# Attention and expert kernel: one burst of value products per batch, with scores and the projection issued ahead of it

## The chip, the cores and the metric

The kernel runs on one core of a Trainium2 chip. The metric is the device time in microseconds (us) of one execution. Three executions of the kernel before gave 748.78, 749.50 and 751.17 us, median 749.5. The profile is of another execution, which took 750.0 us; the span from its first to its last instruction is 748.1 us.

## What is computed

The input is x (64 batches, 64 channels, 256 positions) and a context of the same shape. First cross attention over channels is added to x, then a mixture of experts:

```
q = rotary(Wq @ layernorm(x) + bq);  k = rotary(Wk @ ctx + bk);  v = Wv @ ctx + bv
scores = q @ k.T / sqrt(8)           # 64 batches x 8 heads x 256 x 256, head size 8
x = x + Wo @ (softmax(scores) @ v) + bo
h = layernorm(x)                     # 4096 rows of 256
x = x + routed(h, 2 of 16 experts) + shared(h)
```

All of it is float32; the kernel splits q and k in three bfloat16 parts each, so that the scores come out of bfloat16 matmuls with 72 rows of contraction.

## The kernel before

Each engine has its own program, and every dependency is a semaphore wait written out by hand. All engines run the same loop, `steps`, over a step number r from -8 to 72, and in each step over k = 0 to 7, the eight heads. A step works on several batches at once; `at.has(n)` is true where batch r + n exists. In a full step r:

- TensorE (L1260 on) issues for batch r + 2 the scores S of head k (L1271, two matmuls into one of three banks `bank_s`), and for batch r the transposed scores ST of head k (L1299, into one of two banks `bank_st`). S of a head waits until the reduce of the head that had its bank before is done (L1269, `S_BACK`); ST of head k waits until the exponential of head k - 2 is done (L1297), so ST of head 1 waits for the last exponential of the batch before. The row maxima of batch r + 2, found by VectorE from S, are split by POOL (L679, L682), transposed by TensorE (L1322, once a step), copied by ScalarE (L768) and sent by DMA into the operand of ST as mask rows.
- At k = 4 TensorE projects q (even r) or k (odd r) for batches r + 6 (L1286, into `bank_b`). VectorE applies the rotary tables (L1081, L1083), and POOL splits the result in parts (L666 to L688), which go to DRAM and come back by DMA as the operands of S.
- `values` (L1242) computes the value products of four heads in a burst: 16 matmul instructions of 32 columns each (L1254) into `bank_o`. Each step has two bursts: at k = 2 the second group of batch r - 1, at k = 6 the first group of batch r. After the first of these ScalarE copies `bank_o` (L773), TensorE transposes the copy at k = 4 (L1334), and VectorE normalises it (L1091, L1098) at k = 5.
- Every second step has further products: in even steps the router's logits at k = 2 (L1313), the transpose of the normalised output BT at k = 6 (L1345) and the value projection at k = 7 (L1354); in odd steps the output product WO at k = 1 (L1306) and the transpose of a normalised tile at k = 7 (L1364).
- VectorE reduces S of head k (L1049), does rope at k = 4, and adds the output product to x with its statistics at k = 2 to 4 of odd steps (L1057 to L1063). It also carries the routing operations, at places in the tables `SPREAD` and `DUE`.
- ScalarE computes the exponential of head k (L737) into one of eight buffers `Pr`, and between them the copies out of PSUM and the two normalisations xn (L745, even steps, k = 1) and ring (L755, even steps, k = 6).
- SyncE issues the DMAs of a step, each behind its own waits.

The projections end at r = 57, the scores S at r = 61, the transposed scores at r = 63. In eight or so places of the loop a routing product is placed at k = 6 (`PLACED`). The experts follow from step 64 on, and are not touched.

## Time and profile before

| | us |
|---|---|
| median of three runs | 749.5 |
| profiled execution | 750.0 |
| its span | 748.1 |
| TensorE busy | 703.8 (94%) |
| VectorE busy | 600.2 (80%) |
| ScalarE busy | 467.4 (62%) |
| POOL busy | 419.6 (56%) |

The first transposed scores start at 42.4 us and the last value products at 551.3 us. So about 510 us of the span belong to the attention steps, and the rest to the fill ahead of them and to the experts behind. Each engine's busy time is of the whole span; a matmul's end is modelled, and matmuls overlap in the pipeline, so the distance from one start to the next is what an instruction costs TensorE.

### The profile page before, as it was taken

What the parts mean: (1) busy time and instruction counts of PE and PEld (TensorE: products, weight loads), DVE (VectorE), ACT (ScalarE), POOL (GpSimd) and SP (SyncE); (2) the same over time, 40 slices, a digit from 0 to 9 for tenths busy, and PEclk for the clock granted to TensorE, in tenths of its full rate; (3) what the DMA queues carried; (4) which work ended last, traced back from release to release, by engine and by line L of the source; (5) the groups of instructions that cost most, each with busy time, mean ns of one, the idle gap of its engine ahead of it and who ended that gap; (6) DMA issues with size and microseconds to landing.
All of it is one profiled execution on the core that took longest, in us unless ns stands there. A gap on an engine that the chain in (4) does not pass through costs nothing.

```text
span 748.1 us, 19315 instructions
## 1 busy us (share of the span) xinstructions
PE 703.8 (94%) x6067; PEld 508.1 (68%) x6067; DVE 600.2 (80%) x1580; ACT 467.4 (62%) x1086; POOL 419.6 (56%) x742
## 2 busy tenths in 40 slices
PE   3599999999999999999999999999989889999994
PEld 2366676666667676676666676676558878888883
DVE  6978888899899899989989998998747535466666
ACT  4056777776777777777777777777752255555441
POOL 5544645446657667656756657664345026565663
PEclk9999999999999999999999999999999999999998
DMA  9577444444554555554555455555166335678775
GB/s 285 142 191 205 126 129 120 134 124 122 142 143 131 140 142 147 150 143 131 139 151 148 137 145 134 145 138 144 55 220 200 108 87 170 209 248 276 252 229 167
DMA packets 98514, 118.76 MB, mean 159 GB/s; under 512 B 14317, under 2 KB 82672, under 8 KB 98417
## 3 DMA queue, kind: packets, MB, share of 16 engines
q1 hardware_dynamic: 90400, 99.53, 48.1%
q0 software_dynamic: 6864, 16.93, 6.5%
q8 instruction: 54, 0.88, 0.5%
q10 hardware_dynamic: 1152, 1.07, 0.5%
q14 instruction: 44, 0.35, 0.2%
HBM read 76.80 MB, written 42.11 MB: 159 GB/s over the span
## 4 chain that ended last, share of the span: by engine, by line
PE 81%; DVE 8%; issue 4%; POOL 3%; DMA 2%; ACT 1%; ACTq 1%; DVEq 0%; POOLq 0%; SPq 0%
PE bank_s L1271 15%; PE bank_o L1254 15%; PE bank_st L1299 14%; PE bank_st L1420 8%; PE bank_b L1286 7%; PE bank_s L1438 4%; PE bank_st L1232 3%; DVE M L1049 3%; PE bank_b L1313 2%; PE bank_b L1306 2%; PE bank_a L1354 2%; DVE st L854 2%; PE bank_a L1334 2%; PE bank_b L1345 2%; POOL results L700 1%
## 5 line engine op out<-in xcount | busy, mean ns | idle before, releaser
L1049 DVE TENSOR_REDUCE M<-bank_s 128x2 f32<-128x512 f32 x512 | 339.8, 683 | 41.0 <-PE bank_s L1271 38.4
L737 ACT ACTIVATE Pr<-bank_st 128x512 f32<-128x512 f32 x512 | 297.4, 598 | 117.2 <-PE bank_st L1299 104.6
L1271 PE MATMUL bank_s<-QK 72*128 72x256 bf16 x1024 | 200.6, 279 | 10.7 <-DMA QK<-parts 6.9
L1299 PE MATMUL bank_st<-QK 98*128 98x256 bf16 x1024 | 197.4, 274 | 2.4 <-DMA QK<-Mt 1.0
L666 POOL TENSOR_TENSOR work<-work 128x256 f32<-128x256 f32 x64 | 46.7, 730 | 170.1 <-DVE work L1083 170.1
L1254 PE MATMUL bank_o<-Pr,wide 128*32 128x256 f32 x2048 | 138.0, 385 | 0.0
L1271 PEld LDWEIGHTS bank_s<-QK 72*128 72x128 bf16 x1024 | 92.5, 99 | 66.3 <-DVE M L1049 34.9
L700 POOL DMA_INDIRECT results<-Pr,ids_out x79 | 78.5, 994 | 82.2 <-issue 41.5
L1299 PEld LDWEIGHTS bank_st<-QK 98*128 98x128 bf16 x1024 | 91.5, 98 | 38.9 <-ACT Pr L737 11.1
L1420 PE MATMUL bank_st<-QK,xn 128*128 x316 | 82.0, 382 | 0.6 <-issue 0.4
L1254 PEld LDWEIGHTS bank_o<-Pr,wide 128*32 128x32 f32 x2048 | 55.7, 109 | 34.5 <-issue 13.7
L636 POOL DMA_INDIRECT slots<-ring,slot x64 | 63.8, 997 | 19.9 <-issue 11.2
L1133 DVE TENSOR_TENSOR OT<-work,bank_st 128x128 f32<-128x128 f32 x79 | 22.8, 288 | 59.1 <-ACT work L829 58.9
L1420 PEld LDWEIGHTS bank_st<-QK,xn 128*128 128x128 f32 x316 | 53.9, 190 | 6.0 <-issue 1.7
L1438 PE MATMUL bank_s<-wd,work 128*128 x158 | 47.3, 382 | 0.2 <-DVE Pr L1147 0.2
L669 POOL TENSOR_TENSOR parts_sb<-work 128x256 bf16<-128x256 f32 x64 | 46.6, 728 | 0.0
L671 POOL TENSOR_TENSOR work<-work,parts_sb 128x256 f32<-128x256 f32 x64 | 42.8, 669 | 5.0
L672 POOL TENSOR_TENSOR parts_sb<-work,parts_sb 128x256 bf16<-128x256 f32 x64 | 43.2, 676 | 0.0
L688 POOL TENSOR_TENSOR parts_sb<-work,parts_sb 128x256 bf16<-128x256 f32 x64 | 42.9, 671 | 0.3
L1286 PE MATMUL bank_b<-ctx_kv,w 128*128 128x256 f32 x128 | 35.8, 405 | 3.9 <-DVE work L1083 3.9
L1286 PE MATMUL bank_b<-xn,w 128*128 128x256 f32 x128 | 36.7, 413 | 2.1 <-ACT xn L745 2.1
L1232 PE MATMUL bank_st<-xT_all,parts_sb 128*128 128x128 f32 x256 | 34.8, 279 | 4.1 <-DVE work L979 2.2
(151 smaller groups left out, 1033.3 us busy)
## 6 DMA issues: line engine op xcount, KB each, us to landing
QK<-parts SPq DMA_DIRECT2D x128, 288.0 KB
parts<-parts_sb SPq DMA_DIRECT2D x128, 96.0 KB, 2.3
wide<-slots SPq DMA_DIRECT2D x79, 130.0 KB, 2.4
ctx_kv<-ctx_dram SPq DMA_DIRECT2D x64, 128.0 KB, 2.4
xT_all<-results SPq DMA_DIRECT2D x14, 512.0 KB, 5.1
X<-x_dram SPq DMA_DIRECT2D x8, 512.0 KB, 6.9
parts<-parts_sb SPq DMA_DIRECT2D x64, 64.0 KB, 2.1
QK<-w_gu SPq DMA_DIRECT2D x8, 512.0 KB, 8.7
```

Source lines behind the costliest of these rows:

```text
L636: pool.indirect_dma_start(out=slots, out_offset=bass.IndirectOffsetOnAxis(ap=slot[:, k, n:n + 1], axis=0), in_=ring[:, row, :], in_offset= ...
L666: nc.gpsimd.tensor_tensor(qk[:, h], rc[:, h], rs[:, h], ALU.add).then_inc(s_qk, 1)
L700: pool.indirect_dma_start(out=results, out_offset=bass.IndirectOffsetOnAxis(ap=ids_out[:, at.mod(8, -4):at.mod(8, -4) + 1], axis=0), in_=y ...
L737: nc.scalar.activation(Pr[k][:], bank_st[k % 2][:], ACT.Exp, scale=SCALE).then_inc(s_exp, 1)
L1049: nc.vector.tensor_reduce(M[:, c, 2 * ORDER[k]:2 * ORDER[k] + 2], bank_s[S_BANK[c][k]][:].rearrange("p (a s) -> p a s", a=2), AX.X, ALU.ma ...
L1232: last = nc.tensor.matmul(up_bank[n % 2][:, I * u:I * u + I], sgu[:, c, I * u:I * u + I], xT_all[:, n, c, :], start=(c == 0), stop=(c == 1))
L1254: last = nc.tensor.matmul(bank_o[32 * j:32 * j + 32, 0:T], Vcols[at.odd_pair(off)][:, first:first + 32], Pr[4 * group + j][:, T * chunk:T ...
L1271: last = nc.tensor.matmul(bank_s[S_BANK[at.mod(2)][k]][:, T * t:T * t + T], Q[c][0:KR, ORDER[k], P * t:P * t + P], K[c][0:KR, ORDER[k], :] ...
L1286: last = nc.tensor.matmul(bank_b[:, T * r:T * r + T], w[:, r if even else 2 + r, :], source[:, p, :], start=True, stop=True)
L1299: last = nc.tensor.matmul(bank_st[k % 2][:, T * s:T * s + T], K[c][0:MROW + 2, ORDER[k], P * s:P * s + P], Q[c][0:MROW + 2, ORDER[k], :], ...
L1420: last = nc.tensor.matmul(up_bank[m][:, 0:2 * I], xTs[m][:, c, :], weights(c), start=(c == 0), stop=(c == 1))
L1438: nc.tensor.matmul(down_bank[m][:, 0:T], aT[m][:, 0:P], weights, start=True, stop=True).then_inc(s_d, 1)
```

## The change

It does the following in a full step:

- `values` has no groups any more: at k = 2 all eight heads of batch r - 1 are done in one burst of 32 instructions, behind the exponentials of the whole batch. `s_PV` counts one per batch.
- The exponentials go to 12 buffers in turn, and only the one of head 4 waits for the burst.
- The scores S of batch r + 2 are no longer one per k: heads 0 and 1 at k = 0 and 1, heads 2, 3 and 4 at k = 2 ahead of the burst, head 5 at k = 3, head 6 at k = 4, head 7 at k = 6. The order of banks is shifted to suit.
- The projection moves from k = 4 to k = 2, ahead of these scores; rope on VectorE from k = 4 to k = 1.
- The output product and the router product move from k = 1 and 2 to k = 4, behind the burst; what VectorE does with them moves to k = 6 and 7; the normalisation moves from k = 5 to k = 6, and the aggregation of the statistics to k = 0 of the next step.
- ScalarE's xn moves from k = 1 of even steps to k = 5 of odd ones, ring to k = 5, the copy of BT to k = 6, and the copy of the transposed tile ahead of the exponential of head 0.
- POOL's last part operation moves ahead of the mask operations.

In the steps without a projection (r = 58 on) the places of output and router products, of the normalisation and of the statistics stay as they were.

```diff
-        Pr = [sb(f"Pr{i}", [P, 2 * T]) for i in range(H)]
+        Pr = [sb(f"Pr{i}", [P, 2 * T]) for i in range(12)]
...
-        taken = [((n - 11) % 16 % 3, 1)[(n - 11) % 16 == 15] for n in range(2 * H)]
+        taken = [((n - 8) % 16 % 3, 1)[(n - 8) % 16 == 15] for n in range(2 * H)]
+        AHEAD = ((0,), (1,), (2, 3, 4), (5,), (6,), (), (7,), ())
...
# POOL
+                    wait(pool, s_p2, at.value(1, 7))
+                    nc.gpsimd.tensor_tensor(parts[:, p, h, 2, :], rest[:, h], parts[:, p, h, 1, :],
+                                            ALU.subtract).then_inc(s_pt, 1)
                 if at.has(2):
...
-                if at.has(6):
-                    wait(pool, s_p2, at.value(1, 7))
-                    nc.gpsimd.tensor_tensor(parts[:, p, h, 2, :], rest[:, h], parts[:, p, h, 1, :],
...
# ScalarE
+                if at.r % 2 == 0 and at.has(-6) and at.has(6):
+                    transposed_norm()
                 for k in range(H):
                     if at.has(0):
                         wait(act, s_ST, at.value(8, k + 1))
-                        if k % 4 == 0:
-                            wait(act, s_PV, at.value(2, -1 + k // 4))
-                        nc.scalar.activation(Pr[k][:], bank_st[k % 2][:], ACT.Exp, scale=SCALE).then_inc(s_exp, 1)
-                    if k == 1 and at.r % 2 == 0 and at.has(6):
+                        if k == 4:
+                            wait(act, s_PV, at.value(1, 0))
+                        nc.scalar.activation(Pr[(8 * at.r + k) % 12][:], bank_st[k % 2][:], ACT.Exp, scale=SCALE).then_inc(s_exp, 1)
+                    if k == 5 and at.r % 2 == 1 and at.has(7):
...
-                    if k == 6 and at.r % 2 == 0 and at.has(-4):
+                    if k == (5 if at.has(6) else 6) and at.r % 2 == 0 and at.has(-4):
...
-                        wait(act, s_PV, at.value(2, 0))
+                        wait(act, s_PV, at.value(1, 0))
                         wait(act, s_T1, at.value(1, -1))
                         nc.scalar.activation(O[:], bank_o[:, 0:T], ACT.Copy).then_inc(s_Oe, 1)
...
-                    if k == 7 and at.r % 2 == 0 and at.has(-2):
+                    if k == (6 if at.has(6) else 7) and at.r % 2 == 0 and at.has(-2):
...
# VectorE
+                early = at.has(6)
+                added = 6 if early else 2
                 for k in range(H):
...
+                    if at.r % 2 == 0 and at.has(-4) and k == 0 and at.has(5):
+                        wait(dve, s_st2, at.pairs(-4, add=1))
+                        nc.vector.bn_aggr(mv2[:, at.odd_pair(-4), :], st2[:]).then_inc(s_mv2, 1)
...
-                    if k == 4 and at.has(6):
+                    if k == 1 and at.has(6):
                         h = at.mod(2)
                         wait(dve, s_proj, at.value(1, 7))
...
-                    if k == 5 and at.has(-1):
+                    if k == (6 if early else 5) and at.has(-1):
                         o = bank_a[:, 0:T].rearrange("p (a j e) -> p a j e", a=2, e=32)[:, :, :, 0:2 * D + 2]
...
+                    if k == added and at.r % 2 == 1 and at.has(-3):
+                        wait(dve, s_WO, at.pairs(-3, add=1))
...
# TensorE
-            def values(at, group):
-                off = -group
-                wait(pe, s_exp, at.value(8, 8 * off + 4 * group + 4))
+            def values(at):
+                wait(pe, s_exp, at.value(8, 0))
+                wait(pe, s_Ve, at.pairs(-1, add=1))
+                wait(pe, s_Oe, at.value(1, -1))
+                b = at.mod(2, -1)
+                for group in range(2):
+                    for chunk in range(2):
+                        for j in range(4):
...
             def step(at):
                 for k in range(H):
-                    if at.has(2):
...
-                    if k == 4 and at.has(6):
+                    if k == 2 and at.has(6):
                         p = at.odd_pair(6)
                         if even:
                             wait(pe, s_xn, at.pairs(6, add=1))
-                            held(at, bank_b, (s_lge, at.pairs(-6, add=1), NP))
+                            held(at, bank_b, (s_xte, at.pairs(-6, add=1), NP))
                         else:
                             wait(pe, s_ck[p], at.turns(5, 4, 16, 16))
-                            held(at, bank_b, (s_x2, at.pairs(-3, add=1), NP))
+                            held(at, bank_b, (s_BTe, at.pairs(-3, add=1), NP))
...
+                    for h in AHEAD[k] if at.has(2) else ():
+                        c = at.mod(4, 2)
+                        if h == 0:
+                            wait(pe, s_stk[c], v)
+                        wait(pe, s_red, at.value(8, 16 + h + 1 - S_BACK[at.mod(2)][h]))
...
-                    if not even and k == 1 and at.has(-3):
+                    if not even and k == (4 if at.has(6) else 1) and at.has(-3):
+                        if at.has(6):
+                            wait(pe, s_rope, at.value(1, 7))
...
-                    if even and k == 2 and at.has(-6):
+                    if even and k == (4 if at.has(6) else 2) and at.has(-6):
+                        if at.has(6):
+                            wait(pe, s_rope, at.value(1, 7))
...
                     if k == 2 and at.has(-1):
-                        values(at, 1)
+                        values(at)
...
-                    if k == 6 and at.has(0):
-                        values(at, 0)
```

## Rows read from the trace of the kernel before

**Rows 1.** The page, part 1: busy us, share of the span, instructions

```profile
PE 703.8 (94%) x6067; PEld 508.1 (68%) x6067; DVE 600.2 (80%) x1580; ACT 467.4 (62%) x1086; POOL 419.6 (56%) x742
```

**Rows 2.** Busy time by window: us, PE, PEld, DVE, ACT, POOL, clock, DMA

```profile
100.00:500.00 400.00, 395.75 (x3921) 274.94 (x3920) 368.08 (x840) 295.53 (x626) 251.21 (x493) 1.00 0.52 138
```

**Rows 3.** The waits, 100 to 500 us: us in total, times, longest

```profile
ACT Pr L737 <- PE bank_st L1299: 79.0, 101, 1.7
```

**Rows 4.** The mask transpose L1322, 50 to 510 us: count, durations, first and last start

```profile
L1322 PE MATMUL bank_a<-ident_b,Mb x58: 229/230/231, 54.3 to 509.4; 128*32 128x128 bf16 x58
```

**Rows 5.** Timeline of TensorE: start us, duration us, line, what; an odd and an even step

```profile
324.78 0.23 PE L1322 MATMUL bank_a<-ident_b,Mb 128*32 128x128 bf16 x1
...
331.31 0.38 PE L1271 MATMUL bank_s<-QK 72*128 72x256 bf16 x2
331.72 0.39 PE L1299 MATMUL bank_st<-QK 98*128 98x256 bf16 x2
332.04 0.59 PE L1313 MATMUL bank_b<-wr,xT_all 128*128 128x16 f32 x4
332.56 0.23 PE L1322 MATMUL bank_a<-ident_b,Mb 128*32 128x128 bf16 x1
...
333.58 0.39 PE L1271 MATMUL bank_s<-QK 72*128 72x256 bf16 x2
333.81 0.38 PE L1299 MATMUL bank_st<-QK 98*128 98x256 bf16 x2
...
334.25 1.03 PE L1286 MATMUL bank_b<-xn,w 128*128 128x256 f32 x4
335.12 0.38 PE L1299 MATMUL bank_st<-QK 98*128 98x256 bf16 x2
...
335.56 0.38 PE L1271 MATMUL bank_s<-QK 72*128 72x256 bf16 x2
...
339.57 0.62 PE L1306 MATMUL bank_b<-OT,w 128*128 128x256 f32 x2
340.03 0.38 PE L1271 MATMUL bank_s<-QK 72*128 72x256 bf16 x2
...
340.56 0.23 PE L1322 MATMUL bank_a<-ident_b,Mb 128*32 128x128 bf16 x1
```

**Rows 6.** The chain that ended last: start us, us, engine, tile, line

```profile
284.64 0.86 PE bank_o L1254 x16
```

**Rows 7.** Timeline of ScalarE in the same steps

```profile
330.40 1.26 ACT L737 ACTIVATE Pr<-bank_st 128x512 f32<-128x512 f32 x2 [0.90 <-PE bank_st L1299]
331.56 0.38 ACT L789 ACTIVATE xT_all<-bank_b 128x256 f32<-128x256 f32 x1
331.82 0.60 ACT L737 ACTIVATE Pr<-bank_st 128x512 f32<-128x512 f32 x1
332.30 0.61 ACT L745 ACTIVATE xn<-X,shift,rstd 128x256 f32<-128x256 f32 x1
...
333.74 0.38 ACT L773 ACTIVATE O<-bank_o 128x256 f32<-128x256 f32 x1 [0.21 <-PE bank_o L1254]
...
335.54 1.75 ACT L737 ACTIVATE Pr<-bank_st 128x512 f32<-128x512 f32 x3 [0.71 <-PE bank_st L1299]
```

**Rows 8.** Timeline of VectorE in the even step

```profile
335.32 0.48 DVE L1081 SCALAR_TENSOR_TENSOR work<-bank_b,bias,tab 128x256 f32<-128x256 f32 x1
...
336.11 0.68 DVE L1049 TENSOR_REDUCE M<-bank_s 128x2 f32<-128x512 f32 x1
336.71 0.25 DVE L1091 RECIPROCAL rden<-bank_a 128x16 f32<-128x16 f32 x1
```

**Rows 9.** Timeline of TensorE: the mask transposes of the first steps without a projection

```profile
509.42 0.23 PE L1322 MATMUL bank_a<-ident_b,Mb 128*32 128x128 bf16 x1
...
516.60 0.23 PE L1322 MATMUL bank_a<-ident_b,Mb 128*32 128x128 bf16 x1
```

**Rows 10.** Timeline of TensorE in the fill

```profile
43.05 0.63 PE L1271 MATMUL bank_s<-QK 72*128 72x256 bf16 x2
43.48 0.63 PE L1299 MATMUL bank_st<-QK 98*128 98x256 bf16 x2
```

More of the change, by code:

```diff
@@ L785, in step @@
                         nc.scalar.activation(OT[:], bank_b[:, 0:T], ACT.Copy).then_inc(s_BTe, 1)
-                    if k == 0 and at.r % 2 == 0 and at.has(-6):
-                        wait(act, s_xt, at.pairs(-6, add=1))
-                        nc.scalar.activation(xT_all[:, at.pair(-6)], bank_b[:, 0:2 * P].rearrange("p (c n) -> p c n", c=2),
-                                             ACT.Copy).then_inc(s_xte, 1)
+                    if k == 0 and at.r % 2 == 0 and at.has(-6) and not at.has(6):
+                        transposed_norm()
                     n = shared_tile(at, k)
@@ L1067, in step @@
                         variance(NP - 1)
-                    if k == 2 and at.r % 2 == 0 and at.has(-6):
+                    if k == 1 and at.has(6):
+                        h = at.mod(2)
+                        wait(dve, s_proj, at.value(1, 7))
+                        wait(dve, s_p1, at.value(1, 5))
+                        nc.vector.scalar_tensor_tensor(rc[:, h, :], bank_b[:, 0:T], bias[:, 2 * h:2 * h + 1],
+                                                       tab[:, 0, :], ALU.add, ALU.mult)
+                        nc.vector.scalar_tensor_tensor(rs[:, h, :], bank_b[:, T:2 * T], bias[:, 2 * h + 1:2 * h + 2],
+                                                       tab[:, 1, :], ALU.add, ALU.mult).then_inc(s_rope, 1)
+                    if k == added and at.r % 2 == 0 and at.has(-6):
                         if at.i is None and at.r == 6:
@@ L1103, in step @@
                             ALU.mult).then_inc(s_On, 1)
+                    if k == added and at.r % 2 == 1 and at.has(-3):
+                        pair = at.pair(-3)
+                        xp = X[:, bass.ds(pair, 1), :].rearrange("p a t -> p (a t)")
+                        wait(dve, s_WO, at.pairs(-3, add=1))
+                        nc.vector.scalar_tensor_tensor(xp, bank_b[:, 0:T], beff[:, 0:1], xp,
+                                                       ALU.add, ALU.add).then_inc(s_x2, 1)
+                    if k == added + 1 and at.r % 2 == 1 and at.has(-3):
+                        nc.vector.bn_stats(st2[:], X[:, bass.ds(at.pair(-3), 1), :]
+                                           .rearrange("p a t -> p (a t)")).then_inc(s_st2, 1)
+                    if k == 4 and at.r % 2 == 1 and at.has(-3) and not early:
+                        nc.vector.bn_aggr(mv2[:, at.odd_pair(-3), :], st2[:]).then_inc(s_mv2, 1)
                     n = shared_tile(at, k)
@@ L1114, in step @@
                     if (at.r, k) == (71, 1):
[L1115 removed]
+                        dve.wait_ge(s_PV, NB)
                         dve.wait_ge(s_BT, NP)
@@ L1262, in step @@
                 for k in range(H):
-                    if at.has(2):
-                        c = at.mod(4, 2)
-                        if k == 0:
-                            v = 32 * ((at.r + 2) // 4 + 1)
-                            wait(pe, s_stk[c], v if at.i is None else 32 * at.i + v)
-                        wait(pe, s_red, at.value(8, 16 + k + 1 - S_BACK[at.mod(2)][k]))
-                        for t in range(2):
-                            last = nc.tensor.matmul(bank_s[S_BANK[at.mod(2)][k]][:, T * t:T * t + T],
-                                                    Q[c][0:KR, ORDER[k], P * t:P * t + P], K[c][0:KR, ORDER[k], :],
-                                                    start=True, stop=True)
-                        last.then_inc(s_S, 1)
-                    if k == 4 and at.has(6):
+                    if k == 2 and at.has(6):
                         p = at.odd_pair(6)
@@ L1288, in step @@
                         last.then_inc(s_proj, 1)
+                    for h in AHEAD[k] if at.has(2) else ():
+                        c = at.mod(4, 2)
+                        if h == 0:
+                            v = 32 * ((at.r + 2) // 4 + 1)
+                            wait(pe, s_stk[c], v)
+                        wait(pe, s_red, at.value(8, 16 + h + 1 - S_BACK[at.mod(2)][h]))
+                        for t in range(2):
+                            last = nc.tensor.matmul(bank_s[S_BANK[at.mod(2)][h]][:, T * t:T * t + T],
+                                                    Q[c][0:KR, ORDER[h], P * t:P * t + P], K[c][0:KR, ORDER[h], :],
+                                                    start=True, stop=True)
+                        last.then_inc(s_S, 1)
                     if at.has(0):
```

53 lines of the change are left out of this document (15 added, 38 removed).

## The prediction

> **What bounds the kernel now.** I read the page's busy shares first: TensorE is busy for 94% of the span [rows 1]. The second view is one window over the attention steps, 100 to 500 us: TensorE 395.75 of 400 us, VectorE 368.08, ScalarE 295.53 [rows 2]. The third is who waits for whom there: ScalarE's exponentials wait 79.0 us for TensorE, in 101 places, and no wait of TensorE's comes near that [rows 3]. TensorE seems to be the only bound, and ScalarE seems to have a quarter of its time free. The fourth view says what a step costs: the mask transpose L1322, once a step, is counted 58 times from 54.3 to 509.4 us, so 57 steps take 455.1 us, 7.98 us each [rows 4]. These are the steps that the change rewrites (r = 1 to 57, with projection, scores and values together).
>
> The timelines show what a mean hides. From an even step's transpose to the next (332.56 to 340.56) TensorE never stops: 8.00 us. From an odd one to the next (324.78 to 332.56) it takes 7.78 us, and there a score pair at 331.31 is followed by its successor only at 331.72, 0.41 instead of 0.22 us [rows 5]. That matmul waits for an exponential: the two transposed-score banks are in a ping-pong with ScalarE. So ScalarE is already a second bound, though it idles a quarter of the time: its idle time lies where TensorE does something long between two transposed scores.
>
> **Prices.** I call a head's scores S, its transposed scores ST, its exponential E, its reduce R. On TensorE: S or ST 0.22 us, projection 0.87 (334.25 to 335.12), ST and the transpose of O 0.44 (to 335.56), output product WO 0.46 (339.57 to 340.03). From there S, ST and the switch to 32-column tiles take 0.53 to 340.56, so 0.10 of it for the switch; the router product takes 0.52 with a switch, 0.42 without. From a burst's start, which is 0.01 behind the mask transpose, to the next full matmul (332.57 to 333.58) it is 1.01 [rows 5]. The chain has 0.86 for the 16 instructions alone [rows 6]: the other 0.15 is paid once per burst. On ScalarE [rows 7]: O starts 1.17 after the burst; E starts 0.42 after its ST; an instruction that is ready follows 0.49 behind an E (331.82 to 332.30), and as much behind an xn or a ring copy, which are as long, 0.27 behind a copy (331.56 to 331.82); an E lasts 0.60, and TensorE starts 0.06 after its end (the pair of E from 330.40 ends at 331.66, the ST that waited starts at 331.72). On VectorE [rows 8]: rope starts 1.07 after the projection and takes 0.79 to the next R, whose successor follows 0.60 later; R after its S I take as E after its ST, 0.42.
>
> **The change, part by part.** *One burst instead of two*: 32 instructions take 1.01 + 0.86 = 1.87 us to the next matmul, where two took 2.02, and a switch of 0.10 goes: TensorE's own work falls by 0.25 us a step. Whether the second group flows on as the first does isn't shown; bounds: 0.86 (gapless) and 1.01 (a bubble, gain 0.10 left). I take 0.86, as the chain's row does.
>
> *Three S and the projection ahead of it*: they give VectorE three R and rope (1.8 + 0.8 us) to do during the burst; so VectorE stays fed, and POOL's chain, which waits on rope, starts earlier. S4, at 7.7 in the walk below, waits for R1, which ends at about 6.9 there: nothing. But they also stand between ST1 and ST2, and ST1 waits for E7 of the batch before. Behind ST1, TensorE has projection, S2, S3, S4, ST2, burst, S5, and only then ST3. ScalarE has only E0, E1, E2 and two small copies for that time.
>
> *Output and router products behind it*: same instructions, now between ST4 and ST5, so they delay E5. *POOL's third part operation moved ahead of the mask operations*: its 0.67 us lies before R7's wait; POOL is busy 251 of 400 us [rows 2]; nothing. *12 exponential buffers, moved xn, ring, OT, xT copies, bn_aggr*: the same counts. No DMA is added; SyncE's waits keep their values, and the mask rows leave ScalarE at about 0.8 us after the burst's start and are needed at 5.4: nothing.
>
> **The walk.** Zero is the burst's start. O starts at 1.17 + 0.86 = 2.03. TensorE: S5 1.87, ST3 2.09, S6 2.31, ST4 2.53. E3 starts at 2.51.
> - Even step: router product 2.75, transpose of O 3.17, ST5 3.39, so E5 at 3.81; ring copy 4.30; E6 4.79; OT copy 5.28 (its BT: R5 at 2.30, R6, logits, reciprocal, normalisation end at about 4.2, BT 4.3 to 4.6, no delay up to 0.5 us); E7 5.55, ends 6.15. ST1 6.21, projection 6.43, S2 7.30, S3, S4, ST2 7.96, next burst 8.28.
> - Odd step: WO instead of the router product, so ST5 3.43, E5 3.85, xn 4.34, E6 4.83, E7 5.32 to 5.92. The xT copy then ends at 6.19 and holds the projection to 6.25; S2 7.12, ST2 7.78, next burst 8.10.
>
> The mean is 8.19 us against 7.98, so +0.21 x 57 = +12.0 us: TensorE has 0.25 us less to do and stands idle for half a microsecond. The same walk over the order of before puts the ST of 331.72 at 6.92 us behind its odd transpose, and it lies at 6.94 [rows 5]. VectorE's routing operations and the six placement products (now beside idle TensorE) I cost at 0; bounds from 0 to 0.1 us a step. The six steps behind (r = 58 to 63) have no projection: the first takes 7.18 before (509.42 to 516.60) [rows 9]; the same walk gives 7.4 for such a step and for its successor what it takes now, so 3 x 0.2 = +0.6 us, 0.4 taken since the last two have no S. At the end all eight heads' values stand behind the last exponential, 0.86 us more in the path and a burst less in step 63: +0.5 at most, taken. Start-up: rope comes earlier, bounds -2 to +1, taken 0. Sum: 750.0 (the profiled execution; 748.1 span and 1.9 around it) + 12.9 = 762.9; the median of the runs is 749.5, so **762** in its terms.
>
> **Rivals.**
> 1. *TensorE stays the bound, faster.* If E7 of the batch before ends before TensorE reaches ST1, the step is TensorE's own sum: 7.98 - 0.25 = 7.73, x 57 = -14, 735 us. For: 94% busy. Against: it needs E7's end at under 5.7 us, and the ping-pong gives 5.9 and 6.15; every row it uses is in a steady pattern. 0.09.
> 2. *Both cancel, same.* The waits are 0.2 us shorter in each step than walked (ScalarE taking less behind the burst). 747 to 752. 0.08.
> 3. *VectorE becomes the bound, slower than forecast.* Place: S5 cannot feed R5 before 2.3, and R5, R6, normalisation, x2, R7, R0, R1 must be over before S4. 368 of 400 us busy speaks for it; the idle time before rope in my walk speaks against it. It decides once more than 0.8 us of routing or waiting is added between R5 and R1; at +0.3 us a step on top of my forecast it gives 779 us. 0.12.
> 4. *The clock.* The rows show both levels: at 43.05 us, in the fill, a score pair takes 0.43 us to the next instruction, 1.2 GHz [rows 10]; in the steps it is 0.22, 2.4 GHz. If the new gaps of up to 0.6 us brought the lower level back, TensorE's 7.7 us a step would double and the kernel would be beyond 1000 us. Against: the steps of before have gaps of 0.2 to 0.4 us and the granted clock is 1.00 throughout [rows 2, 5]. 0.01. The Trainium skill ("TensorE: Matmul & The Clock Gate", section "Why this matters for your kernels") warns that idle gaps between bursts of matmuls throw the clock back when they are long; by it gaps as short as these cost nothing.
> 5. That the change doesn't do what it says would show as a second switch or bubble in the burst: +0.15 x 57 = +9, within the range.
>
> **How the numbers follow.** Forecast (slower, ScalarE-paced) 0.70, its own range 753 to 772: 0.15 us a step to either side. The range takes in rival 2's upper half below and most of rival 3 above: 749 to 776. A difference under 0.3% (2.2 us) can't be told from none. Faster 0.10, same 0.08, slower 0.82.
>
> **What would show it.** After the change: L1254's successor with one block of 32 a step; steps of 8.2 to 8.3 (even) and 8.1 (odd); TensorE's busy time down but with waits of ST5 to ST1 on exponentials and BT on VectorE; ScalarE idle in one piece of over 1 us before O. Wrong if steps are under 7.9, if the gap before O is small, or if TensorE waits mostly for VectorE.

## The result and the profile after

The change makes the kernel slower: 775.1 us median of four runs (774.3 to 777.3) against 749.8 for the kernel before, ratio 1.034, 95% interval 1.032 to 1.037. The forecast was 762 us, range 749 to 776, slower with a chance of 0.82. So the direction was right and the time lies at the upper end of the range, but the loss is 25 us where 12.5 were forecast, twice as much. The profiled execution took 775.4 us, its span is 773.6.

The page, part 1, after:

```profile
PE 718.3 (93%) x6067; PEld 513.8 (66%) x6067; DVE 586.9 (76%) x1580; ACT 452.8 (59%) x1086; POOL 424.6 (55%) x742
```

The same instructions as in [rows 1], and TensorE is still called 93% busy. From these shares alone nobody could say what has changed. The window over the attention steps after, with the same columns as [rows 2]:

```profile
100.00:500.00 400.00, 391.31 (x3770) 268.35 (x3770) 341.63 (x815) 271.89 (x602) 244.99 (x473) 1.00 0.50 133
```

TensorE issues 3770 matmul instructions in 400 us instead of 3921, ScalarE 602 instructions instead of 626: 4% fewer steps in the same time, and every engine is less busy. The waits in that window say who holds whom:

```profile
ACT Pr L743 <- PE bank_st L1306: 65.6, 97, 1.3
ACT O L779 <- PE bank_o L1261: 57.1, 48, 1.2
...
PEld bank_st L1306 <- ACT Pr L743: 18.1, 42, 0.5
```

ScalarE waits before the copy of O 1.2 us in each of 48 steps, and TensorE's transposed scores wait for exponentials, 18.1 us in all. In the kernel before the same two rows of this view were

```profile
ACT O L773 <- PE bank_o L1254: 14.8, 50, 0.4
...
PEld bank_st L1299 <- ACT Pr L737: 5.8, 19, 0.3
```

0.3 us a step ahead of O, and a third of the waiting for exponentials. The mask transpose gives the steps:

```profile
L1333 PE MATMUL bank_a<-ident_b,Mb x58: 229/229/231, 57.1 to 530.5; 128*32 128x128 bf16 x58
...
L1333 PE MATMUL bank_a<-ident_b,Mb x64: 229/229/231, 39.5 to 562.0; 128*32 128x128 bf16 x64
```

57 steps take 473.4 us, 8.31 each, where they took 7.98 [rows 4]. This splits the 25.5 us between the two spans into four parts: the transpose of step 1 comes 2.8 us later (57.1 for 54.3), the 57 steps cost 18.3, the four intervals from step 58 to 62 cost 3.3 (31.5 for 28.2; 28.2 is 537.6 less 509.4 before), and what follows 1.1.

The mean of 7.98 hides three kinds of step. Before, an even step took 8.01 us and an ordinary odd one 7.78, but the six odd steps with a routing product (r = 17, 25, ... 57) took 8.57, and six others (r = 13, 21, ... 53) 8.01. After, the ordinary steps take 8.43 and 8.19, the ones with a routing product 8.35 (the last of them 8.70). So an ordinary step lost 0.4 us, and the mean only 0.32, since the steps that were long before lost less or gained.

One even step and the odd one behind it, TensorE's timeline after:

```profile
296.91 0.23 PE L1333 MATMUL bank_a<-ident_b,Mb 128*32 128x128 bf16 x1
296.92 1.95 PE L1261 MATMUL bank_o<-Pr,wide 128*32 128x256 f32 x32
298.80 0.39 PE L1292 MATMUL bank_s<-QK 72*128 72x256 bf16 x2
...
300.31 0.38 PE L1306 MATMUL bank_st<-QK 98*128 98x256 bf16 x2
...
302.66 0.38 PE L1292 MATMUL bank_s<-QK 72*128 72x256 bf16 x2
303.12 0.39 PE L1306 MATMUL bank_st<-QK 98*128 98x256 bf16 x2
303.43 1.10 PE L1281 MATMUL bank_b<-ctx_kv,w 128*128 128x256 f32 x4
304.37 0.82 PE L1292 MATMUL bank_s<-QK 72*128 72x256 bf16 x6
305.03 0.38 PE L1306 MATMUL bank_st<-QK 98*128 98x256 bf16 x2
305.34 0.23 PE L1333 MATMUL bank_a<-ident_b,Mb 128*32 128x128 bf16 x1
...
313.53 0.23 PE L1333 MATMUL bank_a<-ident_b,Mb 128*32 128x128 bf16 x1
```

The burst of 32 is in one piece and the next matmul starts 1.88 us behind its start: the saving of TensorE's work is there as forecast. S1 (302.66) is followed by ST1 only 0.46 us later, at 303.12, since the exponential of head 7 (302.46 in the next rows, 0.60 us long) is not done; behind ST1 stand the projection, three S in a row (6 instructions) and ST2, and then the burst. Even steps take 8.43 us, odd ones 8.19. ScalarE in the same even step:

```profile
297.02 0.60 ACT L743 ACTIVATE Pr<-bank_st 128x512 f32<-128x512 f32 x1 [1.14 <-PE bank_st L1306]
297.51 0.25 ACT L774 ACTIVATE Mt<-bank_a 32x128 bf16<-32x128 bf16 x1
298.96 0.38 ACT L779 ACTIVATE O<-bank_o 128x256 f32<-128x256 f32 x1 [1.19 <-PE bank_o L1261]
...
302.46 1.09 ACT L743 ACTIVATE Pr<-bank_st 128x512 f32<-128x512 f32 x2
```

It is idle for 1.14 us ahead of the exponential of head 2 and for 1.19 us ahead of O. Then the five exponentials of heads 3 to 7 and two other operations (one in odd steps) follow with a single gap of 0.19 us, up to the exponential that ST1 waits for. The row at 302.46 merges it with the exponential of head 0 behind it.

### The profile page after: what moved, and what is told of

It is laid out like the page before. It is cut to its first block, busy times and chain, and to the rows that moved or that the text cites. A ratio compares the mean times of both kernels' runs of the same rounds, so it can differ in the third digit from the quotient of the medians.

```text
span 773.6 us, 19226 instructions
## 1 busy us (share of the span) xinstructions
PE 718.3 (93%) x6067; PEld 513.8 (66%) x6067; DVE 586.9 (76%) x1580; ACT 452.8 (59%) x1086; POOL 424.6 (55%) x742
## 4 chain that ended last, share of the span: by engine, by line
PE 77%; ACT 10%; issue 4%; DVE 3%; DMA 2%; SPq 1%; POOL 1%; ACTq 1%; DVEq 0%; POOLq 0%
PE bank_o L1261 15%; PE bank_st L1306 12%; PE bank_s L1292 12%; PE bank_st L1429 9%; PE bank_b L1281 8%; ACT Pr L743 6%; PE bank_s L1447 4%; PE bank_st L1240 3%; ACT ring L761 2%; PE bank_b L1315 2%; PE bank_a L1345 2%; PE bank_b L1324 1%; DMA QK<-parts 1%; PE bank_b L1373 1%; PE bank_a L1333 1%
## 5 line engine op out<-in xcount | busy, mean ns | idle before, releaser
L1057 DVE TENSOR_REDUCE M<-bank_s 128x2 f32<-128x512 f32 x512 | 331.3, 682 | 52.7 <-PE bank_s L1292 45.1
L743 ACT ACTIVATE Pr<-bank_st 128x512 f32<-128x512 f32 x512 | 289.4, 601 | 96.1 <-PE bank_st L1306 89.2
L1306 PE MATMUL bank_st<-QK 98*128 98x256 bf16 x1024 | 196.9, 273 | 10.8 <-ACT Pr L743 8.0
L1292 PE MATMUL bank_s<-QK 72*128 72x256 bf16 x1024 | 179.9, 277 | 13.4 <-DMA QK<-parts 9.9
L1292 PEld LDWEIGHTS bank_s<-QK 72*128 72x128 bf16 x1024 | 94.3, 99 | 64.0 <-issue 18.5
L1261 PE MATMUL bank_o<-Pr,wide 128*32 128x256 f32 x2048 | 127.1, 387 | 0.0
L1306 PEld LDWEIGHTS bank_st<-QK 98*128 98x128 bf16 x1024 | 87.4, 98 | 51.5 <-ACT Pr L743 29.1
L1261 PEld LDWEIGHTS bank_o<-Pr,wide 128*32 128x32 f32 x2048 | 66.1, 111 | 29.7 <-issue 1.6
L637 POOL DMA_INDIRECT slots<-ring,slot x64 | 63.8, 997 | 21.4 <-issue 12.9
L779 ACT ACTIVATE O<-bank_o 128x256 f32<-128x256 f32 x64 | 24.5, 383 | 81.3 <-PE bank_o L1261 81.3
L683 POOL TENSOR_TENSOR Mb<-M,newton 128x16 bf16<-128x16 f32 x64 | 13.8, 216 | 104.1 <-DVE M L1057 103.9
L1069 DVE SCALAR_TENSOR_TENSOR work<-bank_b,bias,tab 128x256 f32<-128x256 f32 x64 | 30.9, 482 | 29.3 <-PE bank_b L1281 29.3
```

Of the source, the lines that this page charges most:

```text
L637: pool.indirect_dma_start(out=slots, out_offset=bass.IndirectOffsetOnAxis(ap=slot[:, k, n:n + 1], axis=0), in_=ring[:, row, :], in_offset= ...
L743: nc.scalar.activation(Pr[(8 * at.r + k) % 12][:], bank_st[k % 2][:], ACT.Exp, scale=SCALE).then_inc(s_exp, 1)
L1057: nc.vector.tensor_reduce(M[:, c, 2 * ORDER[k]:2 * ORDER[k] + 2], bank_s[S_BANK[c][k]][:].rearrange("p (a s) -> p a s", a=2), AX.X, ALU.ma ...
L1261: last = nc.tensor.matmul(bank_o[32 * j:32 * j + 32, 0:T], Vcols[at.odd_pair(-1)][:, first:first + 32], Pr[(8 * (at.r - 1) + 4 * group + j ...
L1292: last = nc.tensor.matmul(bank_s[S_BANK[at.mod(2)][h]][:, T * t:T * t + T], Q[c][0:KR, ORDER[h], P * t:P * t + P], K[c][0:KR, ORDER[h], :] ...
L1306: last = nc.tensor.matmul(bank_st[k % 2][:, T * s:T * s + T], K[c][0:MROW + 2, ORDER[k], P * s:P * s + P], Q[c][0:MROW + 2, ORDER[k], :], ...
```

## The experiments

Two theories were put against each other. **ScalarE-paced:** the step is the path from the burst over O and the exponentials of heads 3 to 7 to ST1, and from there over projection and three S to the next burst. **VectorE-paced:** the step is the path over the reduces, normalisation and rope. The chips were not equally fast with the kernel before (see the last section), so each result names its time beside it, and steps are read from the traces.

**Half of each exponential, and half of each reduce**, in the changed kernel.

```diff
-                        nc.scalar.activation(Pr[(8 * at.r + k) % 12][:], bank_st[k % 2][:], ACT.Exp, scale=SCALE).then_inc(s_exp, 1)
+                        nc.scalar.activation(Pr[(8 * at.r + k) % 12][:, 0:T], bank_st[k % 2][:, 0:T], ACT.Exp, scale=SCALE).then_inc(s_exp, 1)
...
-                                                    Pr[(8 * (at.r - 1) + 4 * group + j) % 12][:, T * chunk:T * chunk + T],
+                                                    Pr[(8 * (at.r - 1) + 4 * group + j) % 12][:, 0:T],
```

> The changed kernel with the exponential computed for the first half of each head's keys only (256 of 512 columns), and the value products reading that half twice. ScalarE-paced theory: an exponential of 0.60 us becomes one of about 0.38, the walk gives 7.9 to 8.0 us a step instead of 8.31, 748 to 756 us. Rival, VectorE paces the steps: no change, 772 to 777. Rival, TensorE's own work paces them: no change.

```diff
-                                                bank_s[S_BANK[c][k]][:].rearrange("p (a s) -> p a s", a=2),
+                                                bank_s[S_BANK[c][k]][:].rearrange("p (a s) -> p a s", a=2)[:, :, 0:T // 2],
```

> The changed kernel with each maximum taken over the first half of the keys only (a reduce of 256 instead of 512 columns). ScalarE-paced theory: no change in the steps, 770 to 776 us. Rival, VectorE paces the steps: eight reduces of 0.60 us become shorter by about 0.25 each, so 20 us or more below the changed kernel.

The mask transposes of an odd, an even and again an odd step with half exponentials:

```profile
214.09 0.23 PE L1333 MATMUL bank_a<-ident_b,Mb 128*32 128x128 bf16 x1
221.83 0.23 PE L1333 MATMUL bank_a<-ident_b,Mb 128*32 128x128 bf16 x1
229.72 0.23 PE L1333 MATMUL bank_a<-ident_b,Mb 128*32 128x128 bf16 x1
```

Steps of 7.74 and 7.89 us instead of 8.19 and 8.43, a little shorter than the 7.9 to 8.0 expected, and 759.2 us. With half reduces, here an even, an odd and again an even step:

```profile
210.15 0.23 PE L1333 MATMUL bank_a<-ident_b,Mb 128*32 128x128 bf16 x1
218.58 0.23 PE L1333 MATMUL bank_a<-ident_b,Mb 128*32 128x128 bf16 x1
226.76 0.23 PE L1333 MATMUL bank_a<-ident_b,Mb 128*32 128x128 bf16 x1
```

8.43 and 8.18: nothing moved, though VectorE lost a quarter of its work (253 us busy between 100 and 500 us instead of 342); 779.8 us. The exponentials are on the path of a step and the reduces are not: of the two theories the ScalarE-paced one stands. The kernel before took about 790 us beside them, so the totals are not compared with 775.

**The burst alone, and with three S ahead of it**, on the kernel before.

```diff
+            def values(at):          # as in the change: 32 instructions, s_PV once per batch
...
                     if k == 2 and at.has(-1):
-                        values(at, 1)
+                        values(at)
...
-                    if k == 6 and at.has(0):
-                        values(at, 0)
```

> The kernel before with one edit: all eight heads' values in one burst at k = 2; scores, projection and products stay in their old places. Theory (TensorE is gated, not full: the step is set by ScalarE's exponentials and by what TensorE does between two transposed scores): the burst and the projection now lie in two separate gaps, but the transpose of the normalised output has lost the burst that covered the normalisation; the walk gives about 8.7 us for even steps and 7.5 for odd ones, 755 to 765 us in all. Rival (the saved switch and drain of 0.25 us a step are worth their face value, and only the scores and projection ahead of the burst harm): 735 to 742 us.

> The kernel of e1 with heads 2, 3 and 4 of the scores issued ahead of the burst as in the changed kernel, but projection, output and router products in their old places. Theory: 0.65 us more between the last exponential of a batch and the burst, with VectorE fed during it; rope still waits for the projection behind the burst, so the normalisation comes as late as in e1: 760 to 772 us, no better than e1. Rival (VectorE's starving in the burst is the cost): 10 us or more below e1.

e1 has the 12 buffers of the change too; e2 has its order of banks and its table `AHEAD` besides.

They took 845.8 and 875.4 us, 1.073 and 1.105 times the kernel before on that chip (about 790 us), with steps of 8.4 to 12.4 us. Both recorded ranges were missed by far. The rival of e2, that VectorE's starving alone is the cost, is refuted: with three S ahead it is slower still. There VectorE stands 83.5 us, in 40 places between 100 and 500 us, ahead of rope, whose projection is still behind the burst. e1 was measured again:

> The kernel of e1 again (the kernel before with one burst, all else in its old place), beside kernels that share its chip. On its first chip it took 846 us against 791, with steps of 8.75 and 8.38 us up to r = 17 and of 9 to 11 behind. Theory: on a chip where the kernel before takes 750 us the steps stay at 8.75 and 8.38 throughout, 780 to 788 us: the burst in one piece costs more alone than with the moves around it. Rival: e1's cost was the chip's, 755 to 765 us as the first walk said.

806.4 us against 749.6, ratio 1.076 (1.073 to 1.079), so neither theory's number was right. The quiet steps are these:

```profile
207.78 0.23 PE L1321 MATMUL bank_a<-ident_b,Mb 128*32 128x128 bf16 x1
216.16 0.23 PE L1321 MATMUL bank_a<-ident_b,Mb 128*32 128x128 bf16 x1
224.92 0.23 PE L1321 MATMUL bank_a<-ident_b,Mb 128*32 128x128 bf16 x1
```

8.38 (odd) and 8.76 (even). Even steps came as walked (8.7): the transpose of the normalised output has lost the burst that covered the normalisation, and TensorE stands still ahead of it,

```profile
116.27 0.38 PE L1298 MATMUL bank_st<-QK 98*128 98x256 bf16 x2
117.38 0.44 PE L1342 MATMUL bank_b<-ident,On 128*128 128x128 f32 x2 [0.73 <-DVE On L1098]
```

where before it followed the second burst without a gap. Odd steps I had walked at 7.5, 0.9 us too short; the likely reason is that the walk left out that VectorE gets few scores during the burst (it waits 66.3 us for S between 100 and 500 us, in the kernel before 27.5), but no run singles it out. And six of the 57 steps take 10 to 11.2 us: between 100 and 500 us the granted clock is 0.97 in the mean, in the kernel before 1.00. So the burst in one piece is worse alone (1.076 times the kernel before) than in the whole change (1.034), and the moves around it, taken together, are repairs, not costs.

**One head of scores per k** in the changed kernel, the projection still ahead.

```diff
-        AHEAD = ((0,), (1,), (2, 3, 4), (5,), (6,), (), (7,), ())
+        AHEAD = ((0,), (1,), (2,), (3,), (4,), (5,), (6,), (7,))
```

> The changed kernel with one head of scores per k instead of three ahead of the burst; projection ahead, products behind. Theory: the path from the last exponential to the burst is 0.44 us shorter, but VectorE gets only rope and one reduce for the burst, so the normalisation ends 1 us later and BT holds ST7: even steps 8.4 to 8.8 us, odd steps 8.0 to 8.3. Rival (only ScalarE's path counts, the normalisation has slack enough): 7.98 and 7.75.

832.4 us, beside 749.6; quiet steps of 9.18 and 8.69 us, one row of each kind here,

```profile
219.39 0.23 PE L1333 MATMUL bank_a<-ident_b,Mb 128*32 128x128 bf16 x1
228.08 0.23 PE L1333 MATMUL bank_a<-ident_b,Mb 128*32 128x128 bf16 x1
```

(8.69, odd to even), and ten of the 28 even-to-odd steps take 10.8 or more. The direction was expected, the size not. The three S ahead are worth 0.5 to 0.75 us a quiet step to the change. The waits between 100 and 500 us name the way:

```profile
DVE M L1057 <- PE bank_s L1292: 83.5, 126, 1.9
...
PE bank_b L1354 <- DVE On L1094: 29.0, 22, 1.9
```

VectorE waits 83.5 us for scores instead of 30.7, and TensorE stands 1.3 us in each of 22 steps ahead of the transpose of the normalised output, where the changed kernel has one such wait, of 0.6. With the three S but without the projection ahead (e2) the quiet steps were 9.33 and 9.0. So the two belong together: of the orders tried, only the whole change brings the single burst down to 8.43 and 8.19.

**The projection's waits ahead of ST1.**

```diff
-                            wait(pe, s_xn, at.pairs(6, add=1))
-                            held(at, bank_b, (s_xte, at.pairs(-6, add=1), NP))
-                        else:
-                            wait(pe, s_ck[p], at.turns(5, 4, 16, 16))
-                            held(at, bank_b, (s_BTe, at.pairs(-3, add=1), NP))
+                            wait(pe, s_xte, at.pairs(-6, add=1), NP)
...
+                    if k == 1 and at.has(6):
+                        held(at, bank_b, (s_BTe, at.pairs(-3, add=1), NP) if not even else (s_lge, at.pairs(-8, add=1), NP))
+                        if even:
+                            wait(pe, s_xn, at.pairs(6, add=1))
+                        else:
+                            wait(pe, s_ck[at.odd_pair(6)], at.turns(5, 4, 16, 16))
                     if at.has(0):
```

> The changed kernel with the projection's semaphore waits, but for the one on the xT copy, put ahead of ST of head 1 instead of behind it. In the changed kernel the projection starts 0.31 us behind ST1 in even-to-odd steps where back-to-back work takes 0.22. Theory: these waits cost TensorE's queue time when it is not running ahead; the gap becomes 0.22 and these steps 8.33 instead of 8.42 us. Rival: the gap is in the matmuls themselves (another shape of weights): 8.42.

```profile
213.26 0.23 PE L1335 MATMUL bank_a<-ident_b,Mb 128*32 128x128 bf16 x1
221.60 0.23 PE L1335 MATMUL bank_a<-ident_b,Mb 128*32 128x128 bf16 x1
229.77 0.23 PE L1335 MATMUL bank_a<-ident_b,Mb 128*32 128x128 bf16 x1
```

Even-to-odd steps of 8.34 us instead of 8.42, as expected, and 8.17 for the others. But the number came out right by another way than the one on record:

```profile
219.55 0.38 PE L1308 MATMUL bank_st<-QK 98*128 98x256 bf16 x2 [0.16 <-ACT Pr L743]
219.76 1.03 PE L1277 MATMUL bank_b<-ctx_kv,w 128*128 128x256 f32 x4
220.63 0.82 PE L1288 MATMUL bank_s<-QK 72*128 72x256 bf16 x6
```

The gap behind ST1 did close, to 0.21 us, but ST1 itself comes 0.08 later, 6.28 us behind the burst's start (213.27) instead of 6.20 (303.12 less 296.92), so the projection starts where it did, at 6.49 for 6.51. The gain is behind it: S2 follows the projection by 0.87 us instead of 0.94. What is shown is that the place of these waits is worth 0.08 us where TensorE has nothing queued ahead; how, is not. 771.5 us, where the kernel before took 748.9.

**Loads of the expert weights two steps later.**

```diff
-                if at.i is None and 0 <= at.r < 4:
-                    weights(at.r)
+                if at.i is None and 2 <= at.r < 6:
+                    weights(at.r - 2)
```

> The changed kernel with the four loads of expert weights issued in steps 2 to 5 instead of 0 to 3. In the changed kernel's profile TensorE waits 2.95 us at 52.7 us for the operand of the scores (head 0 of step 1), with the DMA queues 0.86 busy by those loads, and issues at half pace behind it. Theory: step 0 to 1 falls from 10.8 to about 8 us and the mask transpose of step 1 comes at 54 to 55 instead of 57.1 us. Rival: the operand is late for its own chain (rope, POOL, two DMAs): no change.

In the changed kernel the second step stands still for the scores' operand:

```profile
52.72 0.39 PE L1292 MATMUL bank_s<-QK 72*128 72x256 bf16 x2 [2.95 <-DMA QK<-parts]
```

With the loads later that wait is gone, step 0 to 1 takes 5.99 instead of 10.79 us and the transpose of step 1 comes at 53.7:

```profile
L1333 PE MATMUL bank_a<-ident_b,Mb x59: 229/229/230, 53.7 to 535.5; 128*32 128x128 bf16 x59
```

771.0 us in all, on the chip of e6, where the transpose of step 1 came at 56.7. So most of the 2.8 us of the fill is this queueing (of the 3.4 us gained on the first profile by step 1, 0.8 is lost again in the two steps behind). That step 0 runs into the loads because it has lost its first burst and is over sooner is my reading; no run shows it. The wait was not the whole cost: behind it, from 53.2 to 55.8 us, pairs of matmul instructions stand 0.43 us apart instead of 0.22, with a granted clock of 0.79 between 52 and 60 us, and in e5 it is 1.00 there.

**The last steps in the old order of scores**, one head per k from r = 58 on.

```diff
-                    for h in AHEAD[k] if at.has(2) else ():
+                    for h in (AHEAD[k] if at.has(6) else (k,)) if at.has(2) else ():
```

> The changed kernel, but in the steps without a projection (r = 58 on) the scores are issued one head per k again. In the changed kernel's profile heads 3 and 4 of the scores wait 0.28 and 0.65 us for VectorE there, and the burst behind them takes 3.29 instead of 1.95 us at a granted clock of 0.66. Theory: with no projection ahead of them, the three scores in a row are what waits, and the clock falls behind that wait: without them the six last steps take 28 to 30 us instead of 31.5, the rest is unchanged. Rival: the tail is long for the single burst alone: 31 to 32.

This is what stood there in the changed kernel:

```profile
529.60 0.39 PE L1292 MATMUL bank_s<-QK 72*128 72x256 bf16 x2 [0.65 <-DVE M L1057]
...
530.51 3.29 PE L1261 MATMUL bank_o<-Pr,wide 128*32 128x256 f32 x32
533.74 0.61 PE L1292 MATMUL bank_s<-QK 72*128 72x256 bf16 x2
```

The step that ends at the mask transpose of 530.50 takes 8.71 us, with the old order 7.35: without the projection between ST1 and S2, the three S in a row reach their banks before VectorE has freed them. (The kernel before takes 8.57 there, it is a step with a routing product. The step is the last of the 57, not one of the intervals from step 58 on.) The theory on record gave the six last steps 28 to 30 us and was not borne out: the four intervals from step 58 on took 33.5 us, one of them 10.4 at a granted clock of 0.84, and the other three 7.79, 7.54 and 7.76. The total was 785.7 us beside 783.2 for the kernel before.

The slow burst is not a matter of those gaps alone. e5 has the same two waits there, to 0.01 us, and behind them

```profile
527.01 0.39 PE L1292 MATMUL bank_s<-QK 72*128 72x256 bf16 x2 [0.65 <-DVE M L1057]
...
527.92 1.95 PE L1261 MATMUL bank_o<-Pr,wide 128*32 128x256 f32 x32
```

a burst of 1.95 us at full clock; so have e6 (waits of 0.17 and 0.65) and the repeat of the changed kernel. The step that begins with this burst takes 7.63 us in these three and 9.27 in the first profile. Why the clock fell in one execution and not in the others, nothing here shows.

**A version that beats both.** In the kernel before, only the odd-to-even steps have idle time, for the exponential of head 0. f1 moves the transpose of the normalised tile from the end of the odd step behind ST of head 0 of the next.

```diff
-                    if not even and k == 7 and at.has(-5):
...
+                    if even and k == 0 and at.has(-6):
...
```

> The kernel before with the transpose of the normalised tile moved from the end of odd steps to the next even step, behind the transposed scores of head 0. In the kernel before, TensorE waits about 0.2 us for the exponential of head 0 ahead of the router product in each odd-to-even step. Theory: the exponential starts 0.2 us earlier and that wait goes, odd-to-even steps of 7.6 instead of 7.78 us, 4 to 6 us off in all (ratio 0.992 to 0.995). Rival (TensorE's own work is the bound in these steps): no change, 7.78.

> f1 again: the kernel before with the transpose of the normalised tile behind ST of head 0 of the next step. Steps of 7.61 instead of 7.78 were seen; on a chip where the kernel before takes 750 us: 744 to 747, ratio 0.993 to 0.996.

```profile
225.63 0.23 PE L1322 MATMUL bank_a<-ident_b,Mb 128*32 128x128 bf16 x1
233.24 0.23 PE L1322 MATMUL bank_a<-ident_b,Mb 128*32 128x128 bf16 x1
```

7.61 us instead of 7.78, as walked, and 746.3 us against 749.6, ratio 0.9961 (0.9946 to 0.9975); on the chip of its first run 778.8 against 783.2, 0.9946 (0.9910 to 0.9981). A small gain, under half a per cent, but clear of the noise on both.

**Scatters behind the burst**, on the kernel before, alone and with f1.

```diff
+                if at.r in STORES and at.r < 59:
+                    wait(pool, s_PV, at.value(2, 0))
```

> The kernel before, where POOL's scatters of a step wait for the first burst of that step (steps 19 to 58). On the chip of c1 the odd steps from r = 19 on, those with scatters beside the first burst, take 8.3 to 10 us instead of 7.78, and O is copied about 2.1 us behind the burst's start instead of 1.17. Theory: burst and scatter side by side are what slows there: with the scatters behind the burst these steps fall back to about 7.8 us and the kernel to 755 to 765 us on such a chip (on one where the kernel before takes 750: no change). Rival: the burst is slow for TensorE's own clock and the scatters have no part in it: no change on either chip.

> f1 and f2 together: the kernel before with the transpose of the normalised tile one place later and the scatters behind the burst. Theory: the gains add, 750 to 760 us where the kernel before takes 783, 744 to 746 where it takes 750. Rival as for f2: only f1's 4 us.

> f2 again, to see it on a chip where the kernel before takes 780 or more: theory (scatter and burst side by side slow each other there) 760 us there; rival (they don't) 783 or more. On a chip where the kernel before takes 750 it tells nothing new: 756.

None of the three ran on a chip where the kernel before is slow, so the question was not answered. Where it is fast, the wait costs: 756.6 and 754.4 us alone, 753.0 with f1, against 749 to 750, since the steps with scatters go from 7.78 to 8.3; so the 744 to 746 us expected of f3 were missed, its edit from f2 being a loss there.

## Why the prediction was right or wrong

The direction and the mechanism were right, ScalarE sets the pace of the changed kernel. What failed is the sum: it added 12.9 us and 25.5 came, since four of its terms were too small, the 57 steps (12.0 forecast, 18.3 measured), the start-up (0, 2.8), the last steps (0.4, 3.3) and the end (0.5, 1.1).

- *TensorE is not full, the exponentials' ping-pong is a second bound.* Right: for the changed kernel e3 against e4 shows it, for the kernel before f1, which takes work from the path to one exponential and gains 0.17 us in every ordinary odd step.
- *32 instructions in 1.87 us to the next matmul.* Right: 1.88. The range's other end, a bubble between the groups, didn't come.
- *The walk.* The mechanism was right: ST5 was walked at 3.39 us behind the burst and lies at 3.39 (300.31), the normalisation had its slack, VectorE had its own. The steps were put at 8.28 and 8.10 and are 8.43 and 8.19. ST1 is where the walk had it (6.20 us behind the burst, walked 6.21). The missing 0.12 us a step, 6.3 of the 12.6 us by which the forecast was short, lie between ST1 and S2. In even steps the projection starts 0.31 us behind ST1 where I took 0.22; in odd steps it starts as walked. In both S2 comes 0.94 behind the projection where I took 0.87 from a row in which TensorE had work queued. The semaphore waits there were priced at nothing, as in the kernel before; e6 shows that their place is worth 0.08 us in the even steps. For the 0.09 us of the odd steps, where e6 gained only 0.02, the cause stays open.
- *+0.21 x 57, walked steps of 8.19 against a mean of 7.98.* The 8.19 is an ordinary pair of steps, the 7.98 a mean that holds the long ones with a routing product; the ordinary pair before is 7.90. The comparison held only because the routing products were also taken to cost nothing beside idle TensorE, and that came out: the mean after, 8.31, is that of an ordinary pair. It was argued and not walked, so part of this is luck.
- *Start-up taken as 0, bounds -2 to +1.* Failed, outside its bounds: +2.8. I priced rope's earlier place and not that the operand of the scores would stand behind the weight loads (e5).
- *The last six steps +0.4.* Failed: +3.3 over the four intervals from step 58 on. Half of it, 1.6 us, is the one burst at reduced clock, and not the order's: e5 and e6 take 29.8 us there for the 31.5. The other 1.6 is: intervals of 7.63, 7.67, 7.63 and 6.9 us (e5) where the kernel before has 7.17, 6.94, 7.17 and 6.90. The forecast had 0.2 us for the first kind and took the second as unchanged, where it costs 0.7. "S4 waits for nothing" holds only with a projection ahead of it: in the step before (e7) S3 and S4 wait 0.28 and 0.65 us, in the second kind S4 waits 0.27. The end behind them cost 1.1 where 0.5 was taken.
- *The clock, 0.01, "gaps as short as these cost nothing".* The rule that the Trainium skill gives ("TensorE: Matmul & The Clock Gate", section "Why this matters for your kernels") fits the steps at 1.00, but the forecast was wrong to make of it that nothing would fall: the burst at 530.51 took 3.29 instead of 1.95 us, at a granted clock of

```profile
530.00:535.00 5.00, 5.00 (x48) 3.04 (x47) 2.13 (x5) 1.49 (x4) 0.00 (x0) 0.66 0.48 122
```

0.66 in the mean of these 5 us, between the levels of 1.2 and 2.4 GHz. No gap of over 0.7 us stands near it. In this profile it is the only such place in the steps from 1 on, in e1b and e8 there are many. The forecast also read the pace in the fill (0.43 us a pair at 43.05) as a granted clock of 1.2 GHz [rows 10]. The pace is there; but the granted clock of the profile reads 1.00 in that stretch, so the row shows half the pace and not the level, and a reading of 1.00 doesn't exclude a lower pace.
- *Rival 1* (TensorE the bound, faster) is refuted by the steps, 8.31 us and not 7.73, and by e3; *rival 3* (VectorE the bound) by e4. That 775 us still lies in the stated range of 749 to 776 is owed to rival 3, for which its upper end was stretched, and so to luck.

The terms of the sum, all of one sign, were each small: 6.3 for the steps, 2.8, 2.9 and 0.6. The forecast's own range of 753 to 772 was too narrow, since it varied the steps alone.

## What to carry to other kernels

Before work is put in one piece, look which engine is fed by the gaps between the pieces: here two bursts of 1 us let a double-buffered exponential go on, and one of 2 us starved it, though its engine was idle a quarter of the time before. A path that alternates between two engines is found by walking one step of the timeline with start-to-start distances. The forecast's walk was good to 2% of a step, its error lay where an engine that was running ahead no longer does; but the walk of e1's odd steps was 0.9 us short. Walk ordinary steps against ordinary steps, and the long ones by themselves. Price the steps at either end of the loop by a walk of their own.

## What the runs showed of the hardware that I had not expected

**The place of satisfied waits is not free** for TensorE when its queue has run dry: moving about six of them ahead of ST1 took 0.08 us off every even step (e6).

**The orders that leave TensorE idle lost the clock too.** In e1b and e8, whose TensorE waits are 0.7 us and more but never 2, 6 and 12 of the 57 steps take 10 to 12.8 us instead of 8.4 to 9.6, and the granted clock between 100 and 500 us is 0.97 and 0.95 in the mean. Here an ordinary and a long step of e8 side by side, with the columns of [rows 2]:

```profile
219.39:228.08 8.69, 7.61 (x76) 5.36 (x76) 7.17 (x17) 5.74 (x12) 5.80 (x12) 1.00 0.63 184
228.08:238.90 10.82, 9.53 (x82) 7.16 (x81) 7.14 (x17) 6.22 (x13) 6.28 (x12) 0.84 0.40 106
```

The kernel before was not profiled on that chip; its time there was 749.6 us as elsewhere, and f1, one move away from it, has no step above 8.4 there. TensorE was busy 92% and 87% of that window in e1b and e8 (89% and 0.95 in e2); every kernel with 96% or more has 1.00. This goes together in all runs; that the one brings the other is not shown.

**The same kernel differs between chips.** The kernel before took 748 to 751 us on the chips of the first measurement, of e5, e6, f2 and f3, and of e1b and e8, and 777 to 796 on two others. It was profiled on one of these, with the changed kernel:

> The kernel before, unedited, profiled on this chip, since its runs beside e1 and e2 took 782 to 796 us where it had taken 749 to 751. Theory: its steps at the full clock are the same 8.01 and 7.78 us, and where it is slower the granted TensorE clock falls in stretches that follow idle time. Rival: every step is longer on this chip, by memory or engine speed.

> The changed kernel, unedited. Theory: steps of 8.42 and 8.19 us as in its first profile wherever the granted clock is 1.00; its time relative to the kernel before is 1.03 where that keeps its clock, and smaller or below 1 on a chip where the kernel before loses it.

They took 781.6 and 785.2 us (median of ten), the latter 1.004 times the 783.2 (median of 23) of the kernel before (1.0015 to 1.007): of the loss of 25 us hardly anything is left. The changed kernel's steps are 8.42 and 8.19 there too. The kernel before has its 8.01 in every even step but one, and its odd steps up to r = 17 are those of the first profile; from r = 19 on the odd ones take 8.1 to 10.3, and the 57 steps together 21 us more. Another 8 to 9 us are lost by both kernels alike behind the last mask transpose, among the experts (219.4 and 219.3 us instead of 210.5 and 211.6). Both theories on record fail for the odd steps: neither is every step longer, nor does the granted clock show a fall, it is 1.00 between 100 and 500 us in the mean. In these steps POOL scatters beside the first burst. In TensorE's record nothing moves, but what reads its results is late:

```profile
264.81 1.08 PE L1254 MATMUL bank_o<-Pr,wide 128*32 128x256 f32 x16
```

and on ScalarE

```profile
266.96 0.38 ACT L773 ACTIVATE O<-bank_o 128x256 f32<-128x256 f32 x1 [1.31 <-PE bank_o L1254]
```

2.15 us behind the burst's start instead of 1.17 [rows 7], with the granted clock at 1.00 in that window. Matmul ends are modelled in the record, and the granted clock read 1.00 in the slow fill too, so a burst at a lower pace would look like this, and so would an operand that came late; which of them it is, and whether the scatters cause it, stays open. The changed kernel scatters in the same steps and keeps its 8.19 there. What is shown is that a ratio measured on one chip need not hold on the next.
